# A two-layer graph network: layer 0's attention scores multiplied graph by graph, in two column halves of the array

## What is computed

```python
# x: (128, 64, 768), adj: (128, 64, 64); 6 heads of 128
h = jnp.maximum(_layernorm(x), 0.0)
q, k, v = _heads(h @ Wq + bq), _heads(h @ Wk + bk), _heads(h @ Wv + bv)
scores = jnp.einsum('bhqd,bhkd->bhqk', q, k) / np.sqrt(128)
bias = jnp.where(adj, 0.0, -9e15)[:, None]
probs = jax.nn.softmax(scores + bias, axis=-1)
x = x + einsum('bhqk,bhkd->bhqd', probs, v).reshape(...) @ Wf + bf
```

## Time and profile before

| | us |
|---|---|
| median of 3 timed runs | 2834.39 |
| lowest and highest of them | 2832.46, 2834.86 |
| span of the profiled execution (first to last instruction) | 2831.0 |
| PE busy in it | 2758.9 |
| DVE busy in it | 2113.9 |
| ACT busy, POOL busy | 998.1, 711.4 |

### The profile page before, as it was taken

The page is one execution under the profiler, slowest core; times in us unless marked ns, Lnnn a source line. Parts: engine busy times, 40 slices in busy tenths (PEclk is TensorE's granted clock), DMA queues, the critical chain, the costliest instruction groups (busy, mean ns, idle before and its releaser), DMA issues.

```text
span 2831.0 us, 53917 instructions
## 1 busy us (share of the span) xinstructions
PE 2758.9 (97%) x22624; PEld 2046.0 (72%) x22624; DVE 2113.9 (75%) x3111; ACT 998.1 (35%) x1374; POOL 711.4 (25%) x537
## 2 busy tenths in 40 slices
PE   6999999999999999999999999999999999999995
PEld 4777777777777777777777777777777777777763
DVE  7777877777777777777777777778777777777777
ACT  5333333233333333333333332333332333332332
POOL 2122222122231222221222221222322222312223
PEclk9999999999999999999999999999999999999997
DMA  7000000000001000000000100000100000000000
GB/s 263 23 18 18 34 33 34 34 10 24 33 34 34 22 12 33 33 34 34 17 17 34 33 34 34 17 17 33 34 34 23 17 28 33 34 34 22 12 23 23
DMA packets 45917, 92.61 MB, mean 33 GB/s; under 512 B 11456, under 2 KB 20672, under 8 KB 45888
## 3 DMA queue, kind: packets, MB, share of 16 engines
q1 hardware_dynamic: 45888, 92.19, 9.5%
HBM read 67.02 MB, written 25.17 MB: 33 GB/s over the span
## 4 chain that ended last, share of the span: by engine, by line
PE 94%; DVE 4%; issue 1%; POOL 0%; DMA 0%; ACT 0%; POOLq 0%; SPq 0%; DVEq 0%; ACTq 0%
PE pair_prj L413 52%; PE pair_prj L423 26%; PE pair_att L437 5%; PE pair_prj L430 3%; PE pair_att L538 3%; PE pair_att L448 2%; PE pair_att L580 2%; PE pair_att L624 1%; DVE w_lo L698 0%; PE pair_att L602 0%; PE pair_att L600 0%; DMA arena<-in_L_gnn_Wq 0%; DVE arena L741 0%; DVE w_top L662 0%; DVE arena L780 0%
## 5 line engine op out<-in xcount | busy, mean ns | idle before, releaser
L413 PE MATMUL pair_prj<-w_hi,arena 128*128 128x512 f16 (+1 forms) x6144 | 1443.7, 326 | 0.0
L413 PE MATMUL pair_prj<-w_lo,arena 128*128 128x512 f16 (+1 forms) x3072 | 1001.0, 326 | 0.0
L413 PEld LDWEIGHTS pair_prj<-w_hi,arena 128*128 128x128 f16 x6144 | 602.6, 98 | 404.6 <-DVE arena L726 4.7
L423 PE MATMUL pair_prj<-arena,w_hi 128*128 128x256 f16 x4608 | 763.2, 273 | 9.4 <-DVE w_lo L698 9.2
L423 PE MATMUL pair_prj<-arena,w_lo 128*128 128x256 f16 x2304 | 628.8, 273 | 0.0
L423 PEld LDWEIGHTS pair_prj<-arena,w_hi 128*128 128x128 f16 x4608 | 449.1, 98 | 61.7 <-DVE w_lo L698 9.6
L413 PEld LDWEIGHTS pair_prj<-w_lo,arena 128*128 128x128 f16 x3072 | 300.8, 98 | 198.2 <-issue 0.3
L1314 POOL TENSOR_TENSOR rstd<-var_eps,minus_half 128x2 f32<-128x2 f32 x64 | 45.2, 706 | 930.9 <-DVE var_eps L718 930.9
L423 PEld LDWEIGHTS pair_prj<-arena,w_lo 128*128 128x128 f16 x2304 | 225.7, 98 | 26.5
L1346 POOL TENSOR_TENSOR arena<-arena 128x768 f32<-128x768 f32 x64 | 116.0, 1813 | 421.6 <-DVE arena L785 421.6
L1341 POOL TENSOR_TENSOR arena<-arena,b_row 128x768 f32<-128x768 f32 x64 | 116.6, 1822 | 375.7 <-DVE arena L763 375.7
(11 more groups left out here) (130 smaller groups left out, 3490.8 us busy)
## 6 DMA issues: line engine op xcount, KB each, us to landing
arena<-in_x SPq DMA_DIRECT2D x64, 768.0 KB, 4.3
out<-arena SPq DMA_DIRECT2D x64, 384.0 KB, 2.3
arena<-in_L_gnn_Wq SPq DMA_DIRECT2D x2, 1152.0 KB, 8.3
arena<-in_L_gnn_Wk SPq DMA_DIRECT2D x2, 1152.0 KB, 11.8
w_hi<-in_L_gnn_Wv SPq DMA_DIRECT2D x2, 1152.0 KB, 13.4
w_lo<-in_L_gnn_Wf SPq DMA_DIRECT2D x2, 1152.0 KB, 16.3
arena<-in_L_gnn_W SPq DMA_DIRECT2D x2, 1152.0 KB, 14.4
arena<-in_L_gnn_H_w SPq DMA_DIRECT2D x2, 1152.0 KB, 13.3
```

Source lines behind the costliest of these rows:

```text
L413: mm = nc.tensor.matmul(pair[:, lo:hi], lhs(a, k), weight(m, k, b)[:, lo:hi], start=(k == 0 and n == 0), stop=(k == KT - 1 and n == 2))
L423: mm = nc.tensor.matmul(pair[:, c * 256:(c + 1) * 256], weight(m, k, a)[:, o:o + P], (ht0_hi, ht0_lo)[b][:, k, :], start=(k == 0 and n == ...
```

## The change

For each tile and head there are two matmuls instead of one, one for each graph: 64 columns of q are loaded and 64 columns of k streamed. The result of graph 0 goes to partitions 0 to 63 of `pair_att[t]` (the lower column half of the array), that of graph 1 to partitions 64 to 127 (the upper half), both at the same 64 elements of the head. The six heads now take 384 elements a partition instead of 768. DVE reads these in one op for each tile, over 128 partitions.

```diff
@@ PE
                         for h in range(H0):
-                            mm = nc.tensor.matmul(pair_att[t][:, h * P:(h + 1) * P], qt[:, h, t * P:(t + 1) * P],
-                                                  kt[:, h, t * P:(t + 1) * P], start=True, stop=True)
+                            for g in range(2):
+                                nodes = slice(t * P + g * N, t * P + (g + 1) * N)
+                                mm = nc.tensor.matmul(pair_att[t][g * N:(g + 1) * N, h * N:(h + 1) * N],
+                                                      qt[:, h, nodes], kt[:, h, nodes], start=True, stop=True)
                         mm.then_inc(s_psum, 1)
@@ DVE
                         dve.wait_ge(s_psum, 2 * i + t + 1)
-                        for g in range(2):
-                            r = slice(N * g, N * g + N)
-                            sc = nc.vector.scalar_tensor_tensor(
-                                p0[r, t * H0:(t + 1) * H0, :],
-                                pair_att[t][r, 0:C].rearrange("p (h n) -> p h n", h=H0)[:, :, r], INV_SQRT_D,
-                                bias0[r, t, :].unsqueeze(1).broadcast_to([N, H0, N]), ALU.mult, ALU.add)
-                        sc.then_inc(s_ready, 1)
+                        nc.vector.scalar_tensor_tensor(
+                            p0[:, t * H0:(t + 1) * H0, :],
+                            pair_att[t][:, 0:H0 * N].rearrange("p (h n) -> p h n", h=H0), INV_SQRT_D,
+                            bias0[:, t, :].unsqueeze(1).broadcast_to([P, H0, N]), ALU.mult, ALU.add)\
+                            .then_inc(s_ready, 1)
```

## The result

The changed kernel takes 2853.5 us in the median (2853.3 to 2854.6), against 2833.4 for the kernel before on the same chip: ratio 1.0071, 95% interval 1.0057 to 1.0086. It is **slower by 0.7%**, 20 us. Forecast was 2801.1, with a range of 2790 to 2848: the measurement lies above the whole range.

A forecast was written before the change was run, and what follows sets the result against it. PE was taken to bound the steady loop. Scores of 1.41 us plus 0.23 for switches against 2.68 save 1.04 a stage, 33.3 us over 32; span 2797.7 plus 3.4 gives 2801.1 us, range 2790 to 2848.

The forecast's parts named there:

- Scores on PE: Scores stage: 48 half-width records, two column halves fully overlapping, take 1.41 us, 1.64 with switches, against 2.68; chance 45%.
- two switches: PE entering and leaving the half-width form at the scores: 0.10 to 0.13 us each, 0.23 us a stage.
- The first rival, halves in turn: Scores matmuls of the two column halves do not overlap: stage 2.91 to 3.05 us, 2842 to 2846 us; 24%.
- loads that aren't hidden: Each half-width scores record pays load and stream, 114.8 ns: 5.74 us a stage without overlap, up to 2932 us; 11%.
- fallen clock: PE's clock falls after the narrow scores matmuls, 31 groups losing 67 us: 2868 us; 7%.
- The sum: 1.04 us saved a scores stage, times 32 is 33.3 us: span 2797.7, median 2801.1 us.
- Group 0: First group, where PE waits 5.86 us for L940: up to 2 us might be gained, counted as 0.
- DVE's pass: DVE's score reads: two ops of 128 x 384 replace four, about 1.15 us less a group, 37 us in all.
- the cover of 5.6 us at L437: Softmax ends with L940 5.6 us before PE reads it at L437; this cover stays, so DVE's saving is off the path.
- What is late next: Just behind the scores, V projection waits for DVE L726: margin 0.4 us; 0.1 short would give back 3 us.
- What bounds the kernel now: Steady loop: PE, busy 2297.0 of 2300 us at full clock, sets the time; other engines matter only if PE waits.
- unhidden loads with the halves in full overlap: Scores stage variant of the unhidden-loads rival: 2.99 us, close to the first rival; the rival as a whole has 11%.

The follow-up runs named there:

- experiment 9: Changed kernel with both graphs' scores multiplied into the lower column half, the upper half's not made, PSUM cleared once at the start; 2844.8 us (one run).
- experiment 3: Kernel before with PE's half alone: 64 x 64 score matmuls written where the diagonal blocks stood, DVE reading in two passes; 2869.1 us, ratio 1.0125.
- experiment 10: Changed kernel with POOL's copy L1355 held until after L931, and all six heads of graph 0 ahead of graph 1's; 2826.4 us (one run).

## Why the prediction was wrong

**Scores on PE: right.** 24 x 58.8 ns for 48 records was forecast as 1.41 us, with 0.23 for two switches 1.64. Measured is 1.55 + 0.09 = 1.64. In the changed kernel's trace the 48 starts are 6 or 7 ns and 51 or 52 ns apart in turn, a pair every 58. The 0.14 by which 1.55 exceeds 1.41 is at the ends, 0.05 at the second pair and 0.10 from the last record to L413; with the 0.09 in front this makes 0.24 for the two switches, where 0.23 was forecast. That the halves overlap was my estimate, since no row of before has matmuls in different column halves; 1.55 us against the 2.94 of experiment 9 shows it. The first rival, halves in turn, was forecast at 2842 to 2846; experiment 9, which has its pace by using one half alone, took 2844.8. The rivals of loads that aren't hidden and of a fallen clock are out: the granted clock is 1.00 in the loop, as in the earlier trace rows, and the loads stay hidden in the narrow form within one half (58 ns a record in experiment 9, with load records of 138 ns) as in the wide one (111.7 with 192).

**The sum: right for PE alone.** With the collisions taken away, by one wait on POOL that the change doesn't have, it is 2800.7 against 2801.1. Group 0, counted as nothing, isn't quite that in the changed kernel: PE's wait for L940 falls from 5.9 to 1.4 us, and the one for L957 rises from 2.3 to 8.4.

**DVE's pass: right in size, wrong in what it triggers.** L912 went from 2.31 to 1.06 us a group, 1.25 less where 1.15 was forecast. The step that failed is the sentence "On the path this is nothing", with the cover of 5.6 us at L437 as its reason. That cover did stay: PE waits for nothing at L437 in the loop. But only this one consumer was looked at. L940 was taken to last its 0.96 us wherever it lies. DVE's earlier phase put it beside POOL's copy, which itself hangs on a DMA (POOL waits 2.67 us for it at L1353, just ahead) and didn't move, and it lasted 0.84 us longer. What was left of DVE's gain no longer kept the shift ahead of the product. The sentence that nothing would be lost without the DVE part falls too: experiment 3 is that kernel, and at 2869.1 us it is 16 us slower than with the part.

**What is late next: wrong.** I looked for waits of PE just behind the scores (L726, 0.4 us of margin, which held) and took the rest of the group to shift as one. It did not: PE, and with it ACT's tanh, came 1.03 us earlier and DVE's statistics 0.47. Between these two stood a margin of 0.33 us, in POOL's order of rstd and product. "No instruction is moved past another on any queue, and no wait is added" was true, and hid that two engines' instructions passed each other in time. This cost 1.81 us a group against the 1.04 won. The sentence in "What bounds the kernel now" that every other engine matters only if PE begins to wait for it was right; the failure was to look for such waits only next to the scores, and to use no row of POOL. The profile of the kernel before had shown the effect: in group 0, beside long ops of POOL (L1324), L921 and L940 take 4.40 and 3.02 us, where their medians are 0.96.

```profile
61.35 4.40 DVE L921 TENSOR_TENSOR p_place<-p_place,max 128x768 f32<-128x768 f32 x1
...
67.95 3.02 DVE L940 TENSOR_TENSOR p_place<-p_place,rinv 128x768 f32<-128x768 f32 x1
```

**Rivals.** The side (slower) had 38%, but for other reasons; none of the rivals was this one, so that this share earns no credit. One sum is at odds with its range: unhidden loads with the halves in full overlap, 2.99 us a stage, come to about 2844, inside the range, while the whole 11% of that rival is counted outside.

## What to carry to other kernels

When a saving changes the phase of one engine against another, look at each pair of DVE and POOL ops on that stretch, not only at waits: which of them read SBUF alone (two tensors in both ops that were held in the loop), how far apart they stand, and which gets there first when one side moves by the gain. Here the costly case was a tiny op (128 x 2) on the critical chain, right behind a POOL op that it waits for. Ordering POOL's long op behind it gave back 46 us, writing it with one input 41, and keeping POOL's copy off the earlier DVE op 53. And if a bounding engine gets faster by what was forecast but the total doesn't follow, ask for the waits of that engine over the loop: one row named this one.

## What the runs showed of the hardware

- Two streams of float32 matmuls in different column halves of the array ran beside each other: 48 records of 64 columns took 1.55 us, against 2.94 in one half (experiment 9). The switch of form came to about 0.14 us on the way in and 0.10 on the way out.
- The 1.55 us were had with the halves in turn in program order. In runs of 12 records of one half it was 2.40 us (experiment 10), with three records at each change of half that found a partner.
- Two DVE ops with two SBUF inputs each, begun 0.07 and 0.48 us behind the start of a POOL op that reads SBUF, were done only when POOL's op was over: the shift, 128 x 2 elements, took 1.75 us, 0.16 without the neighbour and 0.33 as two ops with one input each beside the same neighbour; L940, 128 x 768, took 1.80 us for 0.96. A one-input op of 128 x 768, L772, was held as well, 2.14 us for 0.56.
